# A FiLM transformer block and an expert-choice block: the stretch ahead of the attention loop rebuilt

## The chip, the core and the metric

The kernel runs on one core of a Trainium2 chip. The metric is the device time of one launch in microseconds (us), the median of the runs shown. Smaller is better. The engines are called PE (TensorE), ACT (ScalarE), DVE (VectorE), POOL (GpSimd) and SP (SyncE, which only issues transfers here). Each runs its own instructions in order and waits on semaphores.

## The reference, cut to what matters

```python
# x: (2, 512, 128) float32; cond: (2, 128). Block 0, 128 wide, one head:
h = film(rmsnorm(x, norm1_w), cond, film1_w, film1_b)        # x * (1 + scale) + shift
attn = softmax((h @ q_w + q_b) @ (h @ k_w + k_b).T * D ** -0.5)
x = x + attn @ (h @ v_w + v_b) @ proj_w + proj_b
h = film(rmsnorm(x, norm2_w), cond, film2_w, film2_b)
x = x + gelu(h @ mlp_w1 + mlp_b1) @ mlp_w2 + mlp_b2
# Block 1, 16 heads of 64:
h = ln(x, ln1_g, ln1_b) + silu(cond) @ W_ada.T + b_ada
q, k, v = split(h @ Wqkv.T)                                   # Wqkv: (3 * 16 * 64, 128)
q, k = ln(q, qn_g, qn_b), ln(k, kn_g, kn_b)                   # over the 64 of a head
x = x + attention(q, k, v) @ Wout.T
# then: gate, each of 8 experts takes its 128 best tokens, ln, two layers, scatter-add
```

Since a query or key is layer-normed over its 64 entries, the kernel takes the mean out of the weights: each 64 rows of `Wqkv` of a head are centred once, and only the squares are left to do for each token.

## The kernel before, in words

Everything stays on chip. The 1024 tokens are 8 chunks of 128 (4 for each batch). The program has four parts.

1. Block 0. `x_in` arrives on ACT's queue and right behind it, on the same queue, `wqkv_raw` (1.5 MB); SP issues the rest, the small rows of vectors first, then `film1`, `wq0`, `wk0`, `wv0` and so on. The norm goes: square on ACT (`square`), sum on DVE (`sum_squares`), power -0.5 on POOL (`norm_scale`), product on DVE (`scaled`), transpose on PE (`turn_norm`), FiLM on ACT for batch 0 and on DVE for batch 1 (`into_h`). The same path serves norm 0, 1 and 2. Then q, k and v of both batches, and a loop over the 8 chunks g: `scores0` on PE, maximum on DVE, exponential on ACT, division on DVE, `turn0` on PE, copy on ACT, `mix0` on PE. Then `proj0` of each batch.
2. The weights of block 1 and the MLP of block 0. `make_weights` transposes `Wqkv` and `Wout` in halves of 64 rows (16 transposes for each of four parts m); ACT copies each bank to `w_all` or `wout_T`; DVE sums for the means (`wmean`), POOL subtracts them, DVE casts the whole to `w_hi` (fp32r) and takes the rest `w_lo` for the first half of the heads (POOL does the other half in the loop). Between, PE does the MLP: four `up0` for each batch, each with a gelu on ACT, then `down0`. `block_out` on DVE adds the result to `x_mid` and centres it.
3. The loop of block 1. A piece p is 256 tokens of 2 heads: `project` (three fp32r products in two halves), squares, sums, power -0.5 on POOL, norm, `turn_piece`; a step is 128 query rows of 2 heads: `scores`, maximum, exponential, `turn_probs`, `mix`. Pieces run ahead of the steps; the first five stand ahead of the loop in an order written by hand.
4. Gate, choice by digits, experts, scatter.

PE's order is written out by hand everywhere, and PSUM's eight banks are handed on by semaphores. Sum of squares for norm 1 of batch 1 waits for the projection of batch 1, which waits for `attended0(1)`.

## Time and profile before

| | |
|---|---|
| median of 3 runs | 410.34 us (408.14 to 410.5) |
| the profiled execution | 409.49 us, of which its span (first to last instruction) is 407.8 us |
| PE busy | 365.3 us, 90% of the span |
| ACT, DVE, POOL busy | 268.2, 258.9, 154.9 us |
| mean granted clock of PE | 0.939 of full speed |
| DMA | 9.74 MB |

All times below are from the start of the span. A matmul's row starts when PE begins to read; with a dependent wait the next engine starts some 0.2 us after the end of PE's work, other engines some 0.04 us after each other. Two rows of PE one after the other overlap: the distance of their starts is what the first costs.

### The profile page before, as it was taken

The numbers are of one execution on the slowest core, as the hardware profiler recorded it, in microseconds if no ns is written. First come the engines' busy times: TensorE is split into PE (matmuls) and PEld (weight loads), VectorE is DVE, ScalarE is ACT, GpSimd is POOL, SyncE is SP. The second block draws the span as 40 slices with busy tenths as digits, with TensorE's granted clock in tenths as the row PEclk, the third lists the DMA queues.
The fourth block names the chain that finished last, engine by engine and source line by source line (L and its number), as shares of the span: only waits on it lengthen the run. The fifth ranks groups of instructions, "written<-read, shape, count | busy, mean of one in ns | idle before, by whom it ended". The sixth has DMA issues, their size and how long they took to land.

```text
span 407.8 us, 8743 instructions
## 1 busy us (share of the span) xinstructions
PE 365.3 (90%) x3118; PEld 256.1 (63%) x3118; DVE 258.9 (63%) x596; ACT 268.2 (66%) x655; POOL 154.9 (38%) x159
## 2 busy tenths in 40 slices
PE   0999796676999999999999999999999876799995
PEld 0658555634666676666666766666655555588894
DVE  2466646436876867767768677677686548890333
ACT  2245544349787887887878899978896527256431
POOL 4200431416757546456465464565642011000000
PEclk9999899569999999999999999999999985579999
DMA  8500000000005800000000000000000000000001
GB/s 229 160 2 0 3 0 0 2 0 0 2 3 159 308 0 2 2 2 2 1 2 2 2 3 2 0 2 2 2 2 2 0 2 0 2 2 0 2 0 51
DMA packets 7518, 9.74 MB, mean 24 GB/s; under 512 B 379, under 2 KB 4278, under 8 KB 7478
## 3 DMA queue, kind: packets, MB, share of 16 engines
q1 hardware_dynamic: 5654, 7.11, 5.7%
q10 hardware_dynamic: 1824, 2.10, 1.8%
q8 instruction: 25, 0.41, 0.4%
q14 instruction: 15, 0.12, 0.1%
HBM read 8.68 MB, written 0.52 MB: 23 GB/s over the span
## 4 chain that ended last, share of the span: by engine, by line
PE 81%; DVE 7%; ACT 5%; DMA 2%; issue 2%; POOL 2%; SPq 0%; DVEq 0%; ACTq 0%
PE bank L1318 15%; PE pair L1269 8%; PE pair L1247 8%; PE bank L1070 8%; PE bank L1269 7%; PE bank L1285 6%; PE pair L1285 4%; PE bank L1296 4%; DMA film<-in_L_cond_film_w_dram 2%; PE bank L1210 2%; PE pair L1219 2%; PE bank L1465 2%; PE pair L1305 2%; PE pair L1070 1%; PE pair L1387 1%
## 5 line engine op out<-in xcount | busy, mean ns | idle before, releaser
L424 POOL TENSOR_TENSOR qk_rstd<-qk_ms,minus_half 128x8 f32<-128x8 f32 x32 | 52.5, 1640 | 103.2 <-DVE qk_ms L860 103.2
L1285 PEld LDWEIGHTS bank<-ident,probs 64*128 64x128 f32 x512 | 36.8, 138 | 46.6 <-issue 46.4
L1318 PE MATMUL bank<-probs_T,v_s 128*64 128x256 f32 x512 | 62.3, 385 | 0.6 <-DVE x_att L903 0.6
L872 DVE TENSOR_REDUCE negmax<-pair 128x1 f32<-128x512 f32 x64 | 43.8, 686 | 25.5 <-PE pair L1269 25.5
L598 ACT ACTIVATE probs_T<-bank 128x512 f32<-128x512 f32 x64 | 38.0, 594 | 24.3 <-PE pair L1285 24.1
L589 ACT ACTIVATE probs<-pair,negmax 128x512 f32<-128x512 f32 x64 | 44.0, 687 | 9.6 <-DVE negmax L872 9.4
L1285 PE MATMUL bank<-ident,probs 64*128 64x64 f32 x512 | 43.4, 225 | 2.2 <-DVE probs_T L880 1.3
L1285 PE MATMUL pair<-ident,probs 64*128 64x64 f32 x512 | 45.1, 228 | 0.0
L1318 PEld LDWEIGHTS bank<-probs_T,v_s 128*64 128x64 f32 x512 | 34.1, 136 | 16.5 <-issue 0.8
L880 DVE COPY probs_T<-pair 128x512 f32<-128x512 f32 x64 | 43.7, 682 | 1.2 <-PE pair L1285 1.2
L872 DVE TENSOR_REDUCE negmax<-bank 128x1 f32<-128x512 f32 x64 | 43.6, 683 | 0.0
L589 ACT ACTIVATE probs<-bank,negmax 128x512 f32<-128x512 f32 x64 | 43.6, 694 | 0.0
L1269 PE MATMUL pair<-keys_T,queries_T 64*128 64x512 f32 x128 | 37.1, 656 | 2.0 <-ACT queries_T L581 2.0
L1285 PEld LDWEIGHTS pair<-ident,probs 64*128 64x128 f32 x512 | 36.9, 139 | 0.0
L1269 PE MATMUL bank<-keys_T,queries_T 64*128 64x512 f32 x128 | 36.2, 632 | 0.6 <-ACT probs L589 0.6
L903 DVE TENSOR_TENSOR x_att<-x_att,bank 128x256 f32<-128x256 f32 x32 | 13.5, 422 | 27.9 <-PE bank L1296 27.9
L431 POOL TENSOR_TENSOR qk_n<-qk_raw,qk_rstd 128x512 f32<-128x512 f32 x29 | 30.3, 1043 | 0.0
L1247 PE MATMUL pair<-w_hi,h_hi 128*128 128x384 f32 x64 | 25.3, 396 | 5.0 <-DVE h_lo L841 3.1
L418 POOL TENSOR_TENSOR qk_sq<-qk_raw 128x512 f32<-128x512 f32 x28 | 29.1, 1041 | 0.0
L562 ACT ACTIVATE qk_raw<-pair 128x512 f32<-128x512 f32 x32 | 19.1, 598 | 11.3 <-PE pair L1247 11.3
L437 POOL TENSOR_TENSOR rec_wide<-o_rec,ones 128x256 f32<-128x256 f32 x32 | 19.6, 613 | 14.2 <-DVE o_rec L887 11.4
L894 DVE TENSOR_TENSOR o_T<-bank,rec_T 128x256 f32<-128x256 f32 x32 | 13.6, 425 | 15.2 <-PE bank L1318 15.2
(271 smaller groups left out, 771.6 us busy)
## 6 DMA issues: line engine op xcount, KB each, us to landing
fc_raw<-in_L_cond_fc2s_dram SPq DMA_DIRECT2D x1, 2048.0 KB, 14.9
x_in<-in_x_dram ACTq DMA_DIRECT2D x1, 512.0 KB, 4.1
w<-in_L_cond_mlp_w_dram SPq DMA_DIRECT2D x2, 256.0 KB, 3.6
wout<-in_L_cond_Wout_dram SPq DMA_DIRECT2D x1, 512.0 KB
b_all<-in_L_cond_b2s_dram SPq DMA_DIRECT2D x1, 512.0 KB, 11.1
out_dram<-final SPq DMA_DIRECT2D x2, 256.0 KB, 2.4
film<-in_L_cond_film_w_dram SPq DMA_DIRECT2D x2, 128.0 KB, 5.9
wq<-in_L_cond_q_w_dram SPq DMA_DIRECT2D x1, 64.0 KB, 8.0
```

The lines of the kernel that those rows point to most:

```text
L418: pool.tensor_tensor(qk_sq[:, :, :, :], qk_raw[:, p % 2, :, :, :], qk_raw[:, p % 2, :, :, :], ALU.mult).then_inc(sq_done, 1)
L424: pool.tensor_tensor(qk_rstd[:, :, :].rearrange("p c t -> p (c t)"), qk_ms[:, :, :].rearrange("p c t -> p (c t)"), minus_half[:, 0:8], ALU ...
L431: pool.tensor_tensor(qk_n[:, p % 2, :, :, :], qk_raw[:, p % 2, :, :, :], spread(qk_rstd[:, :, :], [P, 2, 4, HD]), ALU.mult).then_inc(norme ...
L589: act.activation(probs[:, t % 2, h, :], bank[2 * (t % 2) + h][:, :], ACT.Exp, bias=negmax[:, t % 2, h:h + 1], accum_out=row_sum[:, t // 2 ...
L598: act.activation(probs_T[:, r % 2, :, :, at:at + HD], bank[4][:, :].rearrange("p (h k n) -> p h k n", h=2, k=NC), ACT.Copy).then_inc(copie ...
L872: dve.tensor_reduce(negmax[:, t % 2, h:h + 1], bank[2 * (t % 2) + h][:, :], AX, ALU.max, negate=True)\
L880: dve.tensor_copy(probs_T[:, r % 2, :, :, at:at + HD], bank[6][:, :].rearrange("p (h k n) -> p h k n", h=2, k=NC)).then_inc(copied_dve, 1)
L1070: last = pe.transpose(dst[:, n * P:n * P + P], s, ident[:, :])
L1247: last = pe.matmul(in_banks(p)[:, c, 0:W2], h_part[:, at:at + P], w_part[:, g, :], start=(n == 0), stop=(n == 2))
L1269: pe.matmul(bank[2 * (t % 2) + h][:, :], queries_T[rows, i % 2, c * P:c * P + P], keys_T[rows, i % 2, :], start=True, stop=True).then_inc( ...
L1285: last = pe.transpose(bank[(4, 6)[q]][:, n * HD:n * HD + HD], probs[rows, t % 2, n // NC, n % NC * P:n % NC * P + P], ident[rows, rows])
L1318: last = pe.matmul(bank[5][h * HD:h * HD + HD, 0:2 * P], v_s[:, m % 4, k, h * HD:h * HD + HD], probs_T[:, r % 2, h, k, :], start=(k == 0), ...
```

## The change: what it does, and the diff

- The start: `wqkv_raw` is issued after the two squares instead of before them. PE runs 24, 6 and 8 transposes of the identity into a bank that nothing reads (`keep_awake`), around the transpose of the early rows and the FiLM products. DVE does FiLM ahead of the silu.
- PE's order of q, k and v: batch 0 first, then `scores0(0)`, then batch 1's products with `scores0(1)` between.
- The weights: two 64x64 blocks `centring` (identity less 1/64) are made on POOL, and q's and k's parts of `Wqkv` are multiplied by them, so that the weights leave PE turned and centred. Each of three parts (`make_weights(k, m)`, at g = 2, 4 and 5 of block 0's attention loop) fills banks 6 and 7; ACT writes `w_hi` straight from PSUM, DVE writes `w_lo` from PSUM less `w_hi`. `w_all`, `wmean`, POOL's subtraction and the parts of `w_lo` in the loop are gone. `Wout` and `Wgate` are turned after the MLP.
- The MLP: `u0` has its own memory, norm 1 of batch 0 and its MLP start while batch 1's attention ends; `proj0(1)` stands behind `up0(0)`; `down0` goes by k outermost, the last k apart, with `turn_norm(1, 1)` and `turn_norm(2, 0)` ahead of it. The bias `mb0` is added for each batch by itself. A load of ACT's gelu table is called ahead of the last `turned0`.
- Ahead of the loop: `turn_piece(0)` before `project(3)`, `turn_norm(2, 1)` behind `turn_piece(1)`; `qk_ms` and `qk_rstd` have two slots, and `piece_ss(1)` and POOL's second power come before batch 1's norm.
- SP's loads of the experts' weights wait for `Wgate`'s copy and no longer for POOL's last needed `w_lo`.

```diff
+        centring = keep("centring", [P, HD])
...
-        mlp_start = early.at
...
-            sp.wait_ge(w_split, 1 + HP // 2)
+            sp.wait_ge(wout_copied, 3)
...
-            pool.wait_ge(consts, 4)
+            for h in range(2):
+                rows = slice(h * HD, h * HD + HD)
+                pool.wait_ge(consts, 4 + h)
+                pool.tensor_scalar(centring[rows, :], ident[rows, rows], 1.0 / HD, None, ALU.subtract)\
+                    .then_inc(consts, 1)
+            pool.wait_ge(consts, 6)
...
+            def mid_bias(b):
+                at = slice(b * NC, b * NC + NC)
+                pool.wait_ge(norm_done, 3 + b)
+                pool.tensor_tensor(x_mid[:, at, :], x_mid[:, at, :], bias(mb0, NC), ALU.add).then_inc(xmb_ready, 1)
+            for b in range(B):
+                norm_scale(1, b, EPS0)
+                mid_bias(b)
...
-                wait(pool, normed, p)
-                pool.tensor_tensor(qk_rstd[:, :, :].rearrange("p c t -> p (c t)"),
-                                   qk_ms[:, :, :].rearrange("p c t -> p (c t)"),
+                wait(pool, normed, p - 1)
...
-            act.dma_start(wqkv_raw[:, :, :], Wqkv.rearrange("(c p) d -> p c d", p=P)).then_inc(wqkv_in, 16)
...
+            act.dma_start(wqkv_raw[:, :, :], Wqkv.rearrange("(c p) d -> p c d", p=P)).then_inc(wqkv_in, 16)
...
+                act.activation(weight_part(w_hi, n), bank[6 + n % 2][:, :].rearrange("p (g d) -> p g d", d=HD),
+                               ACT.Copy).then_inc(w_high, 1)
...
+            into_h(0)
+            key0(0)
+            exp0(0)
+            key0(1)
+            exp0(1)
+            for g in range(2, TC):
+                exp0(g)
+                turned0(g - 2)
+                if g in (2, 4, 5):
+                    first = {2: 0, 4: 2, 5: 4}[g]
+                    weight_high(first)
+                    weight_high(first + 1)
+            act.wait_ge(mid_ready, 1)
+            square(x_mid, 0)
+            turned0(TC - 2)
+            act.activation(table_call[:, 1:2], minus_half[:, 0:1], ACT.Gelu)
+            turned0(TC - 1)
+            into_h(1)
+            gelu0(0)
+            gelu0(1)
+            act.wait_ge(mid_ready, 2)
+            square(x_mid, 1)
+            for n in range(2, 6):
+                gelu0(n)
             act.wait_ge(norm_in, 1)
             square(xn, 0)
-            act.wait_ge(consts, 2)
+            gelu0(6)
+            gelu0(7)
             act.activation(table_call[:, 0:1], minus_half[:, 0:1], ACT.Exp)
             into_h(2)
-            act.wait_ge(norm_in, 2)
-            square(xn, 1)
+            copy_wout(0)
+            copy_wout(1)
+            act.wait_ge(wT_done, SPLIT_BANKS + 3)
+            act.activation(wgate_T[:, :], bank[5][:, 0:E], ACT.Copy).then_inc(wout_copied, 1)
...
+            def weight_low(n):
+                dve.wait_ge(w_high, n + 1)
+                dve.tensor_tensor(weight_part(w_lo, n), bank[6 + n % 2][:, :].rearrange("p (g d) -> p g d", d=HD),
+                                  weight_part(w_hi, n).bitcast(F32), ALU.subtract).then_inc(w_low, 1)
...
+            query0(0)
+            into_h(0)
+            value0(0)
+            maximum0(0)
+            query0(1)
+            normal0(0)
+            maximum0(1)
+            value0(1)
+            for g in range(2, TC):
+                maximum0(g)
+                normal0(g - 1)
                 if g == 2:
                     late_cols()
                 if g == 4:
                     late_affine()
+                if g in (3, 5, 6):
+                    first = {3: 0, 5: 2, 6: 4}[g]
+                    weight_low(first)
+                    weight_low(first + 1)
                 if g == NC + 2:
                     attended0(0)
-                if g == NC + 4:
-                    batch_out0(0)
+            batch_out0(0)
+            normal0(TC - 1)
+            sum_squares(1, 0)
+            scaled(1, 0, x_mid)
             attended0(1)
-            sum_squares(1, 0)
             batch_out0(1)
-            scaled(1, 0, x_mid)
             sum_squares(1, 1)
             scaled(1, 1, x_mid)
             into_h(1)
-            dve.wait_ge(wT_copied, QK_BANKS)
-            link(dve.tensor_reduce(wmean[:, :, :],
...
+            def keep_awake(n):
+                for _ in range(n):
+                    pe.transpose(bank[7][:, 0:P], ident[:, :], ident[:, :])
+            keep_awake(24)
             pe.wait_ge(early_in, 16 * len(early_loads))
             pe.transpose(bank[0][:, 0:EARLY], early_rows[:, :], ident[0:EARLY, 0:EARLY]).then_inc(cols_T, 1)
+            keep_awake(6)
...
+            keep_awake(8)
...
+                    pe.wait_ge(w_low, SPLIT_BANKS)
...
+            def make_weights(k, m):
+                if m == 2:
+                    pe.wait_ge(wout_in, 32)
+                    pe.wait_ge(gelu0_done, B * HC)
+                else:
+                    pe.wait_ge(wqkv_in, 16)
+                    pe.wait_ge(consts, 6)
+                    pe.wait_ge(k0_ready, 2)
+                    pe.wait_ge(v0_ready, 1)
+                    wait(pe, w_low, 2 * k)
+                for c in range(KC):
+                    for h in range(2):
+                        rows = slice(h * HD, h * HD + HD)
+                        dst = bank[(3 if m == 2 else 6) + h][:, c * HD:c * HD + HD]
+                        if m < 2:
+                            last = pe.matmul(dst, wqkv_raw[rows, KC * m + c, :], centring[rows, :],
+                                             start=True, stop=True)
...
+            def down0(b, ks):
+                pe.wait_ge(mid_ready, b + 1)
+                for k in ks:
+                    pe.wait_ge(gelu0_done, HC * b + k + 1)
+                    for c in range(NC):
+                        last = pe.matmul(bank[(7, 0)[b]][:, c * D:c * D + D],
+                                         u0[:, k, (b * NC + c) * P:(b * NC + c + 1) * P], w20[:, k, :],
+                                         start=(k == 0 and c == 0), stop=(k == HC - 1), skip_group_check=True)
+                if k == HC - 1:
+                    last.then_inc(y0_done, 1)
+            turn_norm(0, 0)
+            pe.wait_ge(qkv_in, 48)
+            pe.wait_ge(affine_ready, 1)
+            pe.wait_ge(h_act, 1)
+            query_key0(0, wq0, bank[3])
+            query_key0(0, wk0, bank[5])
+            turn_norm(0, 1)
+            value0(0)
+            scores0(0)
+            pe.wait_ge(h_dve, 1)
+            query_key0(1, wq0, bank[4])
+            scores0(1)
+            query_key0(1, wk0, bank[6])
+            value0(1)
+            for g in range(2, TC + 2):
                 if g < TC:
                     scores0(g)
-                if 2 <= g < TC + 2:
+                if g == 2:
+                    late_turns()
+                if g == NC + 3:
+                    turn0(g - 2)
+                    proj0(0)
+                else:
                     turn0(g - 2)
                 if g >= 3:
                     mix0(g - 3)
-                if g == 1:
-                    late_turns()
                 if g == 3:
                     late_products()
-                if g == NC + 3:
-                    proj0(0)
+                if g in (2, 4, 5):
+                    make_weights(*{2: (0, 0), 4: (1, 1), 5: (2, 3)}[g])
+            turn_norm(1, 0)
+            mix0(TC - 1)
+            up0(0)
             proj0(1)
-
-
...
+            for n in range(1, HC):
+                up0(n)
+            down0(0, range(HC - 1))
             turn_norm(1, 1)
-            pe.wait_ge(mlp_in, 32)
-            pe.wait_ge(h_act, 2)
...
+            down0(0, (HC - 1,))
+            for n in range(HC, 2 * HC):
                 up0(n)
-                if n == 1:
-                    make_weights(3)
...
+            down0(1, range(HC - 1))
             turn_norm(2, 0)
+            down0(1, (HC - 1,))
+            make_weights(3, 2)
+            pe.transpose(bank[5][:, 0:E], wgate[:, :], ident[0:E, 0:E]).then_inc(wT_done, 1)
             pe.wait_ge(h_split, 1)
-            pe.wait_ge(wT_copied, W_BANKS + 1)
...
             project(0)
             project(1)
-            turn_norm(2, 1)
             project(2)
+            turn_piece(0)
             project(3)
-            turn_piece(0)
             project(4)
             turn_piece(1)
+            turn_norm(2, 1)
             scores(0)
             pe.wait_ge(h_dve, 3)
```

## Rows read from the trace of the kernel before

**Rows 1.** Windows: length, busy of PE, PEld, DVE, ACT, POOL, clock, DMA, GB/s.
```profile
...
70.51:88.05 17.54, 11.16 (x43) 9.89 (x43) 6.33 (x12) 7.39 (x16) 6.09 (x5) 0.62 0.00 1
88.05:101.10 13.05, 9.93 (x64) 5.08 (x65) 7.93 (x16) 9.41 (x25) 5.34 (x5) 0.85 0.00 0
101.10:200.00 98.90, 98.80 (x960) 65.75 (x960) 72.23 (x148) 80.41 (x200) 61.02 (x60) 1.00 0.15 49
...
```

**Rows 2.** Chain that ended last, up to 110: start us, length, what.
```profile
...
2.36 7.73 DMA film<-in_L_cond_film_w_dram
...
23.13 1.11 PE pair L1130 x2
...
73.65 1.64 POOL qk_rstd L424
...
88.05 2.13 PE pair L1269 x4
...
107.12 1.04 PE pair L1247 x6
...
```

**Rows 3.** Timeline of PE: start us, length us, line, operands, count, idle before.
```profile
...
13.62 1.92 PE L1117 MATMUL bank<-h_T,wq 128*128 128x512 f32 x2
...
16.92 1.05 PE L1120 MATMUL pair<-wv,h_T 128*128 128x128 f32 x8
...
31.03 0.60 PE L1070 MATMUL bank<-ident,p 128*128 128x128 f32 x4
31.47 1.06 PE L1145 MATMUL bank<-pT,v 128*128 128x128 f32 x8
32.36 1.02 PE L1130 MATMUL pair<-kT,qT 128*128 128x512 f32 x2
33.22 0.60 PE L1070 MATMUL bank<-ident,p 128*128 128x128 f32 x4
...
43.83 0.66 PE L1192 MATMUL bank<-ident,wqkv_raw 64*128 64x64 f32 x16
...
48.53 3.12 PE L1210 MATMUL bank<-h_T,w 128*128 128x512 f32 x4
...
56.75 3.84 PE L1219 MATMUL pair<-w,u 128*128 128x128 f32 x32
...
70.51 0.41 PE L1247 MATMUL pair<-w_hi,h_hi 128*128 128x384 f32 x1 [3.15 <-DVE h_lo L841]
...
77.33 1.12 PE L1070 MATMUL bank<-ident,xn 128*128 128x128 f32 x4 [3.40 <-DVE xn L723]
...
92.39 1.13 PE L1269 MATMUL pair<-keys_T,queries_T 64*128 64x512 f32 x4
...
```

**Rows 4.** Timelines of ACT, then of DVE, same columns.
```profile
...
4.93 1.15 ACT L481 ACTIVATE sq<-x_in 128x512 f32<-128x512 f32 x2 [1.33 <-DMA x_in<-in_x_dram]
...
36.34 0.69 ACT L512 ACTIVATE p<-bank,soft 128x512 f32<-128x512 f32 x1 [0.92 <-DVE soft L793]
...
7.81 0.69 DVE L723 TENSOR_TENSOR xn<-x_in,rstd 128x512 f32<-128x512 f32 x1
...
35.61 0.69 DVE L793 TENSOR_REDUCE soft<-bank 128x1 f32<-128x512 f32 x1 [0.17 <-PE bank L1130]
...
```

**Rows 5.** Groups by line up to 88: count, busy us, mean ns, idle before.
```profile
...
L404 POOL TENSOR_TENSOR w_all<-w_all,wmean 128x2048 f32<-128x2048 f32 x1 | 3.6, 3619 | 2.1 <-DVE wmean L820 2.1
...
L845 DVE TENSOR_TENSOR w_lo<-w_all,w_hi 128x1536 fp32r<-128x1536 f32 x1 | 1.8, 1759 | 0.0
...
```

**Rows 6.** Timeline of PE after the loop: three banks of transposes.
```profile
...
358.04 2.80 PE L1070 MATMUL bank<-ident,fc_raw 128*128 128x128 f32 x12
...
```

**Rows 7.** Windows of PE after the loop, before and after those transposes.
```profile
...
335.00:358.00 23.00, 17.33 (x145) 12.51 (x144) 19.68 (x96) 10.71 (x20) 2.77 (x4) 0.50 0.00 1
358.00:361.50 3.50, 3.50 (x22) 3.31 (x20) 3.15 (x5) 2.08 (x4) 0.00 (x0) 0.50 0.01 2
361.50:380.00 18.50, 18.50 (x127) 15.80 (x125) 7.13 (x7) 11.79 (x25) 0.00 (x0) 1.00 0.00 1
...
```

More of the change, by code:

```diff
@@ L167, in film_attention_then_expert_choice @@
         w_lo = loop("w_lo", [P, HP, W2], F32R)
+        wqkv_raw = Area(loop.at)("wqkv_raw", [P, WC, D])
         qk_raw = loop("qk_raw", [P, 2, 2, 4, HD])
@@ L906, in _ @@
             piece_ss(0)
-            scaled(2, 1, xn)
+            piece_ss(1)
             piece_norm(0)
-            piece_ss(1)
-            into_h(2)
+            sum_squares(2, 1)
             piece_norm(1)
             piece_ss(2)
+            scaled(2, 1, xn)
+            into_h(2)
             piece_norm(2)
@@ L1197, in _ @@
-            for m in range(3):
-                make_weights(m)
-            turn_norm(1, 0)
-            turn_norm(1, 1)
-            pe.wait_ge(mlp_in, 32)
-            pe.wait_ge(h_act, 2)
-            def up0(n):
-                b, c = n // HC, n % HC
-                if n == HC:
-                    pe.wait_ge(h_dve, 2)
-                wait(pe, gelu0_done, n - 1)
-                pe.matmul(bank[3 + n % 2][:, :], w10[:, c * P:c * P + P], h_T[:, b * N:b * N + N],
-                          start=True, stop=True).then_inc(u0_done, 1)
```

261 lines of the change are left out of this document (96 added, 165 removed).

## The prediction

> **What bounds the kernel now.** I read the windows first. In the loop PE is busy 98.80 of 98.90 us at clock 1.00 [rows 1]: PE bounds it, and nothing here touches PE's work in it. Ahead of it the reader is to see the opposite. From 70.51 to 88.05 PE is busy 11.16 of 17.54 us at a mean clock of 0.62, from 88.05 to 101.10 at 0.85 [rows 1]. So this stretch is bound by chains from engine to engine, and PE's gaps are paid a second time, since the clock falls to its lower level (1.2 GHz) behind them and the products that follow take twice as long. Second the chain of waits: its first long piece is one transfer, `film1`, 7.73 us up to 10.09 [rows 2], with `wqkv_raw` in flight beside it. Third PE's own timeline, for checkpoints that exist in both kernels: first q product 13.62 [rows 3], `scores0(2)` 23.13 [rows 2], first `up0` 48.53, `project(0)` 70.51 [rows 3], `scores(0)` 88.05 [rows 2], `scores(2)` 92.39 [rows 3]. What the change is worth is the shift of the last. Behind it the loop is the same work in the same order; POOL loses one operation in each of four iterations, beside a full PE, which is worth nothing.
>
> **Prices.** On PE at the upper clock, from distances of starts [rows 3]: four transposes 0.44 (31.03 to 31.47), four 128x128 products 0.89 (31.47 to 32.36), a 128x512 product 0.86 (32.36 to 33.22), `down0` 3.7, 16 half transposes 0.55. A `project` is 1.04 [rows 2]. A 512-wide operation is 0.69 on DVE (0.60 if the next is ready) and 0.69 on ACT with its accumulator some 0.2 behind [rows 4]; an ACT copy out of PSUM I take at 0.6. POOL's small power is 1.64 [rows 2].
>
> **Part 1, the start: 13.62 becomes 10.5, -3.1.** With `wqkv_raw` issued behind the squares, `film1` no longer shares the engines with it, and the next limits are `x_in` (4.93 now [rows 4]) and DVE: two sums up to 6.8, the copy of the columns, then `scaled(0, 0)` at 7.81 [rows 4], which waits for POOL. FiLM's three small operations 0.6, `into_h` 0.8 with its wait, and q could start at 10.0 if `x_in` lands at 4.6 or so. Against it stands PE's new work: 24 transposes from 1.6 on. They are 0.21 each at the lower clock (358.04, 12 in 2.6 us [rows 6]), so up to 5.1 us, ending at 6.7, when the copy of the columns wants them; then 6 more, the FiLM products and 8 more. At the upper clock the last 14 take 1.5 and lie half beside DVE; at the lower they take 3.0 and lie on the path, q then at 12.7 or later. ACT issues `wqkv_raw` between its squares and the silu's exponential; nobody on the path waits for that one now that DVE does FiLM first, and the first use of `wqkv_raw` is near 19, so its later landing is covered by 5 us or more (7.7 us for the transfers that now share with it [rows 2]). So -3.1, between -3.6 and 0.
>
> **Part 2, q, k, v: -2.1.** Before, from 13.62 to 23.13, 9.5 us, with two 512 products at twice their price (v starts at 16.92, 3.3 behind 13.62 [rows 3], for what takes 1.7 at the upper clock), the late turns 0.6 and a wait of 0.4. After: q, k, transposes, v, `scores0(0)`, q, `scores0(1)`, k, v, which is six times 0.86, 0.44 and two times 0.89, 7.4 us, no wait in it. If the clock is still low, 1.7 comes back.
>
> The question for both parts is whether transposes lift the clock. In the only long run of bare transposes here, 12 from 358.04 on, the clock was 0.50 before and up to 361.50, and 1.00 behind [rows 6, 7]: only 1.0 us of products stood between, while products ran for 3.3 us from 13.62 before they quickened [rows 3]. I read this as: they count. The Trainium skill, "TensorE: Matmul & The Clock Gate", Part 4 (PE-mode transpose), says the full rate does not engage for transposes, which do not count as PE-busy in the same way; by that rule `keep_awake` is only work in the way, and the rival below is its result. Here row and rule differ, and 7 of 10 go to the row.
>
> **Part 3, the attention of block 0 with the weights inside: -0.5.** Removed ahead of the MLP are three parts of `make_weights` (the row at 43.83 is one [rows 3]) and PE's wait for ACT's copies between them. Added are two parts of 16 centring products and one of 16 transposes (0.55). The trace has no 64-column fp32 product. Lower bound the half transposes, 0.55 for 16; upper bound a 128x128 product each, 0.22, so 3.6. A full product takes two instructions for a transpose's one (x8 against x4 in [rows 3]), and the nearest row is the half transposes, so twice these, 1.1. Walking PE's list from `scores0(2)` to `up0(0)`: six scores 5.2, eight `turn0` 3.5, eight `mix0` less one behind the norm's transpose 7.1, late turns and products 1.3, weights 2.75, `proj0(0)` 0.9, `turn_norm(1, 0)` 0.4: 21.2. The waits: the third part needs `w_low(3)`, which DVE reaches after `maximum0(5)` and the division, 1.5 beyond PE's other work; `proj0(0)` needs `w_low(5)` and `attended0(0)` behind it, 0.8; batch 0's norm (sum 0.7, POOL 1.3, product 0.7) shows 1.0; small ones 0.4. Queued behind them on PE are the scores of the next chunk, and ACT's `w_high` keeps `exp0` of the next chunk waiting. Sum 24.9 against 25.4. Per step DVE now has 1.4 and ACT 1.35 of PE's 2.19, and six `w_low` of 0.6 (1.76 for three in [rows 5]) and six `w_high` of 0.5 are spread over three of the steps: cover enough, if the order holds. Bounds -1.6 and +5.
>
> **Part 4, the MLP: 22.0 becomes 18.0, -4.0.** Work of PE: eight `up0` 6.9, `down0` twice 7.4, `proj0(1)` 0.9, two norms' transposes 0.9, `Wout` and gate 0.7: 16.8, and waits 1.2. What goes: 0.6 of v's weights, 1.3 because the first two `up0` came at the lower clock (3.1 for four instructions [rows 3] against 1.7), and of the wait of 3.15 for `h_lo` [rows 3] all but 0.7, since norm 2 of batch 0 now runs beside batch 1's `down0` and `split_h(0)` stands ahead of `block_out(1)` on DVE. POOL's 3.62 over the weights and DVE's work around it [rows 5] go too; they were beside PE and are worth nothing themselves. ACT's two table loads move into the path's neighbourhood: the gelu load stands ahead of `turned0(7)`, covered by PE's `turn0(7)`, `mix0(6)` and the norm's wait; uncovered it costs 1.3.
>
> **Part 5, five pieces ahead of the loop: 17.5 becomes 11.4, -6.1.** PE's work is five `project` 5.2, three times 0.44: 6.5. The waits are 4.9: `turn_piece(0)` is behind square, sum, POOL's 1.64 and the norm, 1.7; then 1.6, 0.9 and 0.7. Before, the transposes for norm 2 of batch 1 stood second in PE's list and cost 3.40 [rows 3], as POOL did 1.64 [rows 2] of the first piece ahead of them; `project(2)` to `project(4)` and both first `scores` then ran at the lower clock. New on DVE is `piece_ss(1)` ahead of the first norm; POOL's second power follows its first without a gap. The added waits, `project(1)` for `att_added` and the first two `turn_piece` for the copies of `Wout` and `Wgate`, have long been met when PE comes there in the walk; late by x they would cost x, with `project(2)` and all of the list behind them.
>
> **Part 6, the first scores: 4.34 becomes 3.0, -1.3**, the clock alone.
>
> **Sum.** -3.1 - 2.1 - 0.5 - 4.0 - 6.1 - 1.3 = -17.1. A walk with every wait at its least is too good; and in part 5 PE idles 4.9 of 11.4 us, so the clock may fall once. I allow 2.0: a fall doubles two to three pieces, 2 to 3 us, in some half of the cases, and 0.1 here and there is lost. So -15.1: 409.5 for the profiled execution (407.8 of it span) becomes 394.4. The median of the runs stands 0.85 above that execution, so the forecast is 395.
>
> **Rivals.**
> - Transposes don't lift the clock. For it the rule above, and that FiLM's products and eight transposes between 10.09 [rows 2] and 13.62 did not speed the first q. Against it rows 6 and 7. Price: q at 13.0 to 13.6 instead of 10.5, 1.7 and more in part 2, and one more fall ahead of the loop: +6, 401. Chance 0.25.
> - The weights bind the attention loop. Each part goes PE 1.1, two `w_high` 1.0, two `w_low` 1.3, and the next use of banks 6 and 7 waits for it. If centring products cost 0.22 each (+5), or each of three rounds is waited for in full (3.4 each against 2.3 counted for all): +5 to +8, 402. For it: the two waits that the walk already finds; against it: 0.8 us of slack for ACT and DVE in each step. Chance 0.15.
> - Slower: the clock stays low through the whole of block 0. PE's work there is 21.2 and 16.8 us, each microsecond at the lower level costs one more, so it decides once more than 19 us of it run low; all of it gives 395 + 38 = 433. It would need a rule by which small and half-height work keeps the level down, as in the digits' part, where PE is busy 17.33 of 23.00 at 0.50 [rows 7]. Against it: products as wide as here lifted the clock each time. Chance 0.02.
> - The shift is given back in the loop or the tail. The experts' loads come earlier, PE is full there anyway. Chance 0.03, 405 to 410.
>
> **Chances and range.** The forecast has 0.55 (389 to 399). For 8 in 10 the range takes in the first two rivals: 389 to 403. A median of this kernel can tell 1%, 4 us, from no change. Faster by over 1%: 0.94, within 1%: 0.04, slower: 0.02.
>
> **What the profile after would show.** First q product near 10.5 and `film1` gone from the chain of waits; the 512 products 0.86 apart from the first on; 25 us from `scores0(2)` to `up0(0)` with one wait of PE for DVE's `w_lo` of 1.5; clock 1.00 from 40 to 60; `project(0)` near 61, `scores(0)` near 73, and from there the same distance to the end as before. Wrong would be: first 512 products 1.7 apart (rival one), centring products over 0.1 each or PE waiting over 3 us for `w_lo` (rival two), or a clock of 0.5 in the windows before `scores(0)`.

## The result, and the profile after

The changed kernel takes 395.75 us (median of 4 runs, 395.59 to 397.12) where the kernel before took 410.29 beside it: a ratio of 0.967, with a 95% interval of 0.963 to 0.971. Its profiled execution took 395.64, 393.9 of it span, against 407.8 of span before. The sum in the prediction was 394.4 for that execution, the forecast 395.

Windows of the changed kernel, from the first `up0` to `project(0)`, from there to the first `scores`, and of the loop (columns as in [rows 1]):

```profile
...
44.71:62.63 17.92, 17.45 (x113) 12.55 (x114) 8.41 (x14) 9.16 (x15) 3.68 (x5) 1.00 0.00 1
62.63:74.02 11.39, 7.54 (x42) 6.31 (x43) 7.74 (x15) 8.35 (x20) 6.38 (x5) 1.00 0.00 0
...
77.41:200.00 122.59, 119.26 (x1156) 79.17 (x1157) 88.87 (x182) 100.17 (x250) 70.93 (x68) 1.00 0.12 40
...
```

PE is busy 7.54 of 11.39 us in the five pieces ahead of the loop, at clock 1.00, where [rows 1] has 11.16 of 17.54 at 0.62. The work is the same five pieces, so the 3.6 us that PE's busy time fell by is the clock, and PE idles 3.85 instead of 6.4. The loop itself is the same: from the first mix to the last it takes 221.60 before and 221.73 after (325.97 less 104.37, 311.10 less 89.37).

PE's timeline of the changed kernel, whose rows answer to [rows 3]:

```profile
...
1.57 5.20 PE L1089 MATMUL pair<-ident 128*128 128x128 f32 x24 [1.57 <-POOL minus_half L366]
...
7.94 1.07 PE L1089 MATMUL pair<-ident 128*128 128x128 f32 x8
8.85 0.60 PE L1081 MATMUL pair<-ident,xn 128*128 128x128 f32 x4
10.41 1.10 PE L1131 MATMUL bank<-h_T,wq 128*128 128x512 f32 x2 [0.96 <-ACT h_T L484]
11.34 1.02 PE L1131 MATMUL bank<-h_T,wk 128*128 128x512 f32 x2
...
17.86 1.02 PE L1145 MATMUL pair<-kT,qT 128*128 128x512 f32 x2
...
26.93 2.00 PE L1191 MATMUL pair<-centring,wqkv_raw 64*128 64x64 f32 x32
28.86 1.12 PE L1145 MATMUL bank<-kT,qT 128*128 128x512 f32 x2
...
32.72 0.71 PE L1196 MATMUL pair<-ident,wqkv_raw 64*128 64x64 f32 x16 [1.40 <-DVE w_lo L791]
...
37.66 1.16 PE L1170 MATMUL pair<-wp,oT 128*128 128x128 f32 x8 [0.54 <-DVE oT L796]
...
43.09 0.66 PE L1081 MATMUL pair<-ident,xn 128*128 128x128 f32 x4 [0.72 <-DVE xn L721]
...
44.71 1.10 PE L1207 MATMUL bank<-h_T,w 128*128 128x512 f32 x2
...
62.63 0.41 PE L1279 MATMUL pair<-w_hi,h_hi 128*128 128x384 f32 x1 [0.46 <-DVE h_lo L854]
...
65.36 0.44 PE L1279 MATMUL pair<-w_hi,h_hi 128*128 128x384 f32 x1 [0.41 <-ACT v_s L562]
...
68.03 0.66 PE L1081 MATMUL bank<-ident,qk_n 128*128 128x128 f32 x4 [1.35 <-DVE qk_n L877]
...
71.16 0.45 PE L1279 MATMUL pair<-w_hi,h_hi 128*128 128x384 f32 x1 [1.42 <-ACT v_s L562]
...
74.02 1.13 PE L1303 MATMUL pair<-keys_T,queries_T 64*128 64x512 f32 x4 [0.68 <-ACT queries_T L577]
...
77.41 1.13 PE L1303 MATMUL pair<-keys_T,queries_T 64*128 64x512 f32 x4 [0.81 <-ACT probs L585]
...
```

The reader is to see three things. The first two 512 products start 0.93 apart (10.41, 11.34), and the eight idle transposes ahead of them take 0.91 to the next start (7.94, 8.85), 0.11 each: both at the upper clock, where [rows 3] has 3.3 us for two products. The centring products cost 1.93 for 16 (two instructions each, 26.93 to 28.86). And PE still waits ahead of the loop, but never for more than 1.42, where it waited 3.15 and 3.40 before [rows 3].

The steps of the prediction against this trace (us):

| from, to | before | predicted | after |
|---|---|---|---|
| start to first q | 13.62 | 10.5 | 10.41 |
| to `scores0(2)` | 9.51 | 7.4 | 7.45 |
| to `up0(0)` | 25.40 | 24.9 | 26.85 |
| to `project(0)` | 21.98 | 18.0 | 17.92 |
| to `scores(0)` | 17.54 | 11.4 | 11.39 |
| to `scores(2)` | 4.34 | 3.0 | 3.39 |
| to the end of the span | 315.41 | 315.4, and 2.0 allowed | 316.49 |

### The profile page after: what moved, and what is told of

Its sections match the earlier page's. It is cut to its first block, busy times and chain, and to the rows that moved or that the text cites. A ratio compares the mean times of both kernels' runs of the same rounds, so it can differ in the third digit from the quotient of the medians.

```text
span 393.9 us, 8921 instructions
## 1 busy us (share of the span) xinstructions
PE 365.6 (93%) x3188; PEld 260.2 (66%) x3188; DVE 256.0 (65%) x596; ACT 267.2 (68%) x656; POOL 148.6 (38%) x157
## 4 chain that ended last, share of the span: by engine, by line
PE 83%; DVE 7%; ACT 5%; issue 2%; POOL 1%; DVEq 0%; POOLq 0%; ACTq 0%
PE bank L1352 15%; PE pair L1303 8%; PE pair L1279 7%; PE bank L1303 7%; PE bank L1081 7%; PE bank L1319 6%; PE pair L1319 4%; PE bank L1330 4%; PE bank L1207 2%; PE bank L1499 2%; PE pair L1089 2%; PE pair L1081 2%; PE pair L1339 2%; PE pair L1215 2%; PE pair L1421 1%
## 5 line engine op out<-in xcount | busy, mean ns | idle before, releaser
L1303 PE MATMUL pair<-keys_T,queries_T 64*128 64x512 f32 x128 | 36.1, 641 | 2.4 <-ACT queries_T L577 1.6
L1303 PE MATMUL bank<-keys_T,queries_T 64*128 64x512 f32 x128 | 35.2, 617 | 0.6 <-ACT probs L585 0.6
L1279 PE MATMUL pair<-w_hi,h_hi 128*128 128x384 f32 x64 | 24.3, 379 | 2.3 <-ACT v_s L562 1.8
L428 POOL TENSOR_TENSOR rec_wide<-o_rec,ones 128x256 f32<-128x256 f32 x32 | 19.6, 612 | 14.2 <-DVE o_rec L897 11.4
```

What stands on the lines that cost most here:

```text
L1279: last = pe.matmul(in_banks(p)[:, c, 0:W2], h_part[:, at:at + P], w_part[:, g, :], start=(n == 0), stop=(n == 2))
L1303: pe.matmul(bank[2 * (t % 2) + h][:, :], queries_T[rows, i % 2, c * P:c * P + P], keys_T[rows, i % 2, :], start=True, stop=True).then_inc( ...
```

## The experiments

All changes are to the changed kernel unless the text says that they are to the kernel before. Intervals are those of the ratio to the kernel before, whose median beside these runs was 408.9 to 410.2; so the ratios are what to compare (the change alone: 0.967). The checkpoints of each profiled execution, from PE's timeline (first mix is the first product of probabilities with values in the loop):

| run | first q | `scores0(2)` | `up0(0)` | `project(0)` | `scores(0)` | first mix | span | ratio |
|---|---|---|---|---|---|---|---|---|
| before | 13.62 | 23.13 | 48.53 | 70.51 | 88.05 | 104.37 | 407.8 | 1 |
| after | 10.41 | 17.86 | 44.71 | 62.63 | 74.02 | 89.37 | 393.9 | 0.967 |
| no_awake | 10.56 | 19.67 | 46.52 | 64.44 | 75.82 | 91.18 | 395.4 | 0.974 |
| awake_24 | 10.25 | 19.38 | 46.23 | 64.15 | 75.54 | 90.89 | 395.4 | 0.974 |
| wqkv_first | 15.10 | 24.21 | 51.06 | 68.98 | 80.36 | 95.71 | 399.5 | 0.979 |
| before_wqkv | 11.12 | 21.16 | 46.49 | 68.80 | 86.11 | 102.40 | 406.5 | 0.996 |
| before_both | 10.88 | 18.81 | 44.15 | 64.96 | 82.00 | 98.28 | 402.3 | 0.990 |
| plain_weights | 9.98 | 17.43 | 41.70 | 59.63 | 71.02 | 86.37 | 389.7 | 0.957 |
| late_third | 10.86 | 18.31 | 43.52 | 61.44 | 72.83 | 88.19 | 392.1 | 0.960 |
| reordered | 10.06 | 17.51 | 44.37 | 62.29 | 72.67 | 88.03 | 392.5 | 0.963 |
| old_order | 10.44 | 17.89 | 44.74 | 62.67 | 81.42 | 97.73 | 401.3 | 0.983 |
| mlp_behind | 10.13 | 17.58 | 51.49 | 70.11 | 81.52 | 96.88 | 400.5 | 0.985 |
| both_orders | 10.62 | 18.07 | 43.27 | 61.20 | 71.58 | 86.93 | 391.6 | 0.960 |
| awake_moved | 10.12 | 17.57 | 42.77 | 60.69 | 72.05 | 87.40 | 390.6 | 0.960 |

Two things must be known to read it. Among the seven profiled executions with the same start (after, plain_weights, late_third, reordered, old_order, mlp_behind, both_orders) the first q wanders from 9.98 to 10.86, so distances between checkpoints say more than positions. It goes with how soon the clock rises inside the 24 idle transposes: they take 4.39, 4.55 and 4.70 us where the first q comes at 9.98, 10.06 and 10.13, and 5.20 to 5.38 where it comes at 10.41 to 10.86. The earliest of them, plain_weights:

```profile
...
1.57 4.39 PE L1089 MATMUL pair<-ident 128*128 128x128 f32 x24 [1.57 <-POOL minus_half L366]
...
8.37 0.66 PE L1081 MATMUL pair<-ident,xn 128*128 128x128 f32 x4
...
```

Here the norm's transposes start at 8.37, where the changed kernel's start at 8.85 behind the eight idle ones. The distances repeat to 0.02 where nothing was touched: `up0(0)` to `project(0)` is 17.92 or 17.93 in ten of the runs. And behind the first mix the time to the end is between 303.2 and 304.7, by where the clock falls after the loop (end of the section on the prediction).

### Do idle transposes lift the clock?

**no_awake.**

```diff
-            keep_awake(24)
...
-            keep_awake(6)
...
-            keep_awake(8)
```

> The changed kernel without its 38 idle transposes at the start (24, 6 and 8). Theory, transposes lift the clock: the norm's transposes no longer stand behind the eight (they started at 8.85 though xn was ready at 8.25), so the first q product comes 0.4 to 0.6 earlier, near 9.9; but the first two to three 512 products are 1.7 apart instead of 0.86 and v's eight small ones slower as well: +2 to +2.6 by the second chunk's scores. Net +1.5 to +2: 397.3 to 397.8 us. Rival, the transposes do nothing for the clock and the products quicken by themselves: 512 products 0.86 apart from the first on, and the kernel is 0.5 faster than with them, 395.3.

Measured 398.05 us, ratio 0.974 (0.970 to 0.977). PE's timeline of it:

```profile
...
8.48 1.12 PE L1081 MATMUL pair<-ident,xn 128*128 128x128 f32 x4 [0.52 <-DVE xn L721]
10.56 2.05 PE L1128 MATMUL bank<-h_T,wq 128*128 128x512 f32 x2 [0.96 <-ACT h_T L484]
12.39 1.78 PE L1128 MATMUL bank<-h_T,wk 128*128 128x512 f32 x2
14.01 0.60 PE L1081 MATMUL bank<-ident,xn 128*128 128x128 f32 x4
...
```

The two products start 1.83 apart and the next comes 1.62 behind, against 0.93 and 0.86. From first q to `scores0(2)` it is 9.11 against 7.45: 1.66 for the clock, the 1.7 of the prediction's part 2. The first q itself isn't earlier, as was expected (9.9), for the norm's four transposes now take 1.12 instead of 0.60 and end as late. So the first rival falls, and the transposes are worth 1.8 us at the first mix and 2.3 to 2.6 in the medians and ratios.

The prediction weighed a rule of the Trainium skill, "TensorE: Matmul & The Clock Gate", Part 4 (PE-mode transpose), by which the full rate does not engage for transposes. This pair of runs speaks against it: the same products run at about twice the pace behind the 38 transposes. So do the transposes themselves, 0.21 each at first and 0.11 each in the burst of eight.

**awake_24.** Only the first 24.

```diff
-            keep_awake(6)
...
-            keep_awake(8)
```

> The changed kernel with the first 24 idle transposes only, without the 6 and the 8 behind. Theory, the 24 do the lifting and the other 14 are work in the way: the norm's transposes start at 8.3 instead of 8.85, q 0.5 earlier, products 0.86 apart from the first on: 395.2 us. Rival, the clock needs the others too: between 6.8 and 10 PE has only 1 us of work, the clock is down again at the first q product, and 1.7 comes back: 397.

397.79 us, ratio 0.974 (0.969 to 0.978): the rival. Its timeline:

```profile
...
8.63 0.66 PE L1081 MATMUL pair<-ident,xn 128*128 128x128 f32 x4 [0.56 <-DVE xn L721]
10.25 1.33 PE L1129 MATMUL bank<-h_T,wq 128*128 128x512 f32 x2 [0.96 <-ACT h_T L484]
11.38 1.91 PE L1129 MATMUL bank<-h_T,wk 128*128 128x512 f32 x2
13.08 1.06 PE L1081 MATMUL bank<-ident,xn 128*128 128x128 f32 x4
...
```

At 8.63 the clock is up (0.66 for four transposes), in the middle of q it falls, and the k product takes 1.70 to the next start. All that the 24 had bought is lost: it is 9.13 to `scores0(2)`, as with none. The 14 behind them are needed.

### What is the place of the Wqkv load worth?

**wqkv_first**, the load issued ahead of the squares, all else as changed:

```diff
             act.dma_start(x_in[:, :, :], x.rearrange("b (c p) d -> p (b c) d", p=P)).then_inc(x_loaded, 16)
+            act.dma_start(wqkv_raw[:, :, :], Wqkv.rearrange("(c p) d -> p c d", p=P)).then_inc(wqkv_in, 16)
             act.wait_ge(x_loaded, 16)
...
-            act.dma_start(wqkv_raw[:, :, :], Wqkv.rearrange("(c p) d -> p c d", p=P)).then_inc(wqkv_in, 16)
```

> The changed kernel with the Wqkv load issued ahead of the squares again, as before the change. Theory, the two loads shared the DMA engines and film1 was the path: film1 lands near 10 again, the first q product is at 13.3 instead of 10.4, and PE has nothing between 7.7 and 10, so the clock is down for the first two 512 products: +2.9 and +1.7, 400.3 us. Rival A, the transposes before and behind FiLM keep the clock up over that gap: +2.9 alone, 398.6. Rival B, the order of issue is worth nothing, the transposes took the gain: 395.7, q at 10.4.

400.9 us, ratio 0.979 (0.975 to 0.983), near the 400.3 of the theory. But the first q comes at 15.10, 1.8 later than the 13.3 expected, and `film1` is not what was late. Timeline and windows:

```profile
...
8.69 0.27 PE L1093 MATMUL pair<-ident,early_rows 7*128 7x7 f32 x1 [2.73 <-DMA early_rows<-in_L_cond_k_b_dram]
...
11.34 1.95 PE L1089 MATMUL pair<-ident 128*128 128x128 f32 x8
...
15.10 2.05 PE L1131 MATMUL bank<-h_T,wq 128*128 128x512 f32 x2 [0.96 <-ACT h_T L484]
...
```

```profile
...
6.00:8.70 2.70, 0.01 (x1) 0.01 (x1) 0.92 (x2) 0.13 (x1) 1.96 (x4) 0.91 1.05 298
8.70:15.00 6.30, 5.38 (x23) 4.59 (x23) 2.34 (x9) 0.98 (x2) 1.30 (x2) 0.50 0.73 173
...
```

In this execution PE waited for the small rows (`early_rows`, 8.69; 5.24 to 5.36 is when PE could read them in before_wqkv and no_awake, and 6.03 in the kernel before, which issues the `Wqkv` load as early), and not for `film1` behind them. Why they came so much later than at 6.03 is not shown. PE had nothing for 2.7 us, the granted clock went to 0.50, and the other 14 transposes ran at half pace. So the transposes alone buy nothing: first q to `scores0(2)` is 9.11, as without them.

**before_wqkv**, the opposite edit to the kernel before (the load moved behind the squares), and **before_both**, that and the three calls of `keep_awake`.

> The kernel before, with only the Wqkv load issued behind the two squares. Theory: film1 lands near 7.5, the first q product comes 2.9 to 3.2 earlier (10.6), still at the lower clock, and all that follows shifts by the same: 410.3 - 3.1 = 407.2 us. Rival: the weights' later landing or the order on DVE (silu ahead of the first norm) eats part of it: 408 to 409.

> The kernel before with the Wqkv load issued behind the squares and with the 24, 6 and 8 transposes at the start, nothing else. Theory, the transposes lift the clock: beside the 3.1 of the load, the first two 512 products are 0.86 apart instead of 1.7, -1.7, less 0.4 because the eight stand in the norm's way: 410.3 - 4.4 = 405.9 us. Rival: transposes do nothing for the clock: 407.2 to 407.7, first products 1.7 apart.

408.17 us, ratio 0.996 (0.994 to 0.999), where 407.2 was expected: the rival's range. And 404.56, ratio 0.990 (0.986 to 0.993). Their first q products:

```profile
...
11.12 1.91 PE L1117 MATMUL bank<-h_T,wq 128*128 128x512 f32 x2
...
```

```profile
...
10.88 1.02 PE L1126 MATMUL bank<-h_T,wq 128*128 128x512 f32 x2
...
```

The load alone brings the first q 2.50 forward, but from there to `scores0(2)` it takes 10.04 instead of 9.51, the clock being down for longer, and 1.97 is left at the first mix, 1.3 of span. So the load alone is worth 0.7 us by the medians and 1.5 by the ratio, not 3.1. With the transposes it is 4.32 at `scores0(2)` and 6.09 at the first mix; nearly all of the growth is the clock in two stretches (`up0(0)` to `project(0)` 20.81 instead of 21.98, `project(0)` to `scores(0)` 17.04 instead of 17.54). The 4.3 of the medians lies near the 4.4 expected.

### What did the centring products cost?

**plain_weights**, queries and keys not centred:

```diff
-                            last = pe.matmul(dst, wqkv_raw[rows, KC * m + c, :], centring[rows, :],
-                                             start=True, stop=True)
+                            last = pe.transpose(dst, wqkv_raw[rows, KC * m + c, :], ident[rows, rows])
```

> The changed kernel with plain transposes in place of the 64 centring products (so queries and keys are not centred: that part of the computation is left out). Theory, the products are on PE's path and were mis-sized: two times 1.93 becomes two times 0.55, and the stretch from the second chunk's scores to the first up0 falls from 26.85 to 24.1 or so; 2.5 us less for the kernel, 393.2. Rival, DVE and ACT (six w_hi, six w_lo) are what binds and PE would only wait longer for them: under 1 us less, with larger waits of PE for w_lo and for the quotient.

391.82 us, ratio 0.957 (0.953 to 0.961), and 24.27 from `scores0(2)` to `up0(0)` instead of 26.85.

```profile
...
19.33 0.71 PE L1191 MATMUL pair<-ident,wqkv_raw 64*128 64x64 f32 x16
19.97 1.12 PE L1145 MATMUL bank<-kT,qT 128*128 128x512 f32 x2
...
29.71 0.71 PE L1195 MATMUL pair<-ident,wqkv_raw 64*128 64x64 f32 x16 [1.40 <-DVE w_lo L791]
...
```

16 transposes are 0.64 and 16 products 1.93; twice 1.29 is 2.58, the whole difference in this stretch. The median fell by 3.9, more than the 2.5 expected: at the first mix it is 3.00, of which 0.43 is this run's start, and the rest lies behind the loop. PE's wait for `w_lo` stays at 1.40: the products are on the path with their full length, and ACT and DVE follow them.

### Where does PE wait, and does an order help?

**late_third.**

```diff
                     turn0(g - 2)
+                if g == NC + 2:
+                    make_weights(2, 3)
                 if g >= 3:
                     mix0(g - 3)
...
-                if g in (2, 4, 5):
-                    make_weights(*{2: (0, 0), 4: (1, 1), 5: (2, 3)}[g])
+                if g in (2, 4):
+                    make_weights(*{2: (0, 0), 4: (1, 1)}[g])
```

> The changed kernel with the third part of the weights moved in PE's list behind scores0(6) and turn0(4), where it stood ahead of them and waited 1.40 us for DVE's w_lo. Theory, that wait is filled by 1.3 us of work: up0(0) 1.0 to 1.4 earlier, 394.6 us. Rival, ACT's w_hi and DVE's w_lo of that part come later by as much and the wait moves to the batch's projection and the mix behind it: no change, 395.7.

393.66 us, ratio 0.960 (0.957 to 0.964). From `scores0(2)` to `up0(0)` 25.21, 1.64 less, more than the 1.0 to 1.4 expected: the 1.40, and 0.35 of the wait for the projection of batch 0 (0.54 in the changed kernel), less 0.11 elsewhere:

```profile
...
33.17 0.71 PE L1196 MATMUL pair<-ident,wqkv_raw 64*128 64x64 f32 x16
...
36.46 1.16 PE L1170 MATMUL pair<-wp,oT 128*128 128x128 f32 x8 [0.19 <-DVE oT L796]
...
```

**reordered.** PE turns piece 1 ahead of `project(4)`; ACT copies piece 3 ahead of piece 0's affine step.

```diff
-            for p in range(2, 4):
-                piece_raw(p)
-                piece_square(p)
-                piece_affine(p - 2)
+            piece_raw(2)
+            piece_square(2)
+            piece_raw(3)
+            piece_affine(0)
+            piece_square(3)
+            piece_affine(1)
...
-            project(4)
             turn_piece(1)
+            project(4)
```

> The changed kernel with three steps exchanged ahead of the loop: PE turns piece 1 ahead of project(4), and ACT copies piece 3 out of PSUM ahead of both affine steps of piece 0. By the trace PE waited 1.42 for that copy and 0.68 for the queries. Theory, the path from there into the loop is this chain: scores(0) at 72.7 instead of 74.0 and all behind it 1.3 us earlier, 394.4. Rival, the loop's first products wait for something else (POOL's small powers, the exponentials): scores(0) comes earlier and the loop's first mix stays where it was, 395.7.

394.31 us, ratio 0.963 (0.959 to 0.967). `project(0)` to `scores(0)` 10.38 instead of 11.39, and the first mix 1.34 earlier, of which 0.35 is this run's start:

```profile
...
70.35 0.44 PE L1281 MATMUL pair<-w_hi,h_hi 128*128 128x384 f32 x1 [0.41 <-ACT v_s L562]
...
72.67 1.13 PE L1305 MATMUL pair<-keys_T,queries_T 64*128 64x512 f32 x4 [0.55 <-ACT queries_T L577]
...
```

The wait for `v_s` fell from 1.42 to 0.41. 1.0 of the expected 1.3 came.

**old_order.** The order of before in the five pieces:

```diff
-            project(2)
-            turn_piece(0)
-            project(3)
-            project(4)
-            turn_piece(1)
-            turn_norm(2, 1)
+            turn_norm(2, 1)
+            project(2)
+            project(3)
+            turn_piece(0)
+            project(4)
+            turn_piece(1)
```

and on POOL `norm_scale(2, 1)` ahead of `piece_scale(1)`, on ACT `square(xn, 1)` ahead of the pieces, on DVE the sums and norms as before.

> The changed kernel with the order of before in the five pieces ahead of the loop, on PE, POOL, DVE and ACT (batch 1's norm first, its transposes second in PE's list). Theory, the order carries most of part 5: PE waits some 5 us for the norm with nothing behind it, the clock falls, and the projects and the first scores run at half rate: scores(0) 5 to 6 later, its distance to scores(2) back to over 4; 402 us. Rival, part 5 came from the clock that was up already when PE got there and not from the order: 396 to 397.5.

403.23 us, ratio 0.983 (0.978 to 0.988):

```profile
...
70.71 1.12 PE L1081 MATMUL bank<-ident,xn 128*128 128x128 f32 x4 [5.71 <-DVE xn L721]
71.47 0.67 PE L1279 MATMUL pair<-w_hi,h_hi 128*128 128x384 f32 x1
...
81.42 2.08 PE L1303 MATMUL pair<-keys_T,queries_T 64*128 64x512 f32 x4 [1.11 <-ACT queries_T L577]
...
```

PE waits 5.71 for the norm, the clock falls, and `scores(0)` is 18.75 behind `project(0)`, where it was 17.54 before the change. In this stretch PE idles 8.69 instead of 3.85 and is busy 10.06 instead of 7.54, at a mean clock of 0.73. The first mix comes 8.36 later. So the order on the four engines, which was undone only as a whole, carries all of part 5; the rival, a clock that is up already when PE gets there, would have left it near 11.4. It is worth more here than the difference of the two kernels, since the norm of batch 1 starts later against `project(0)` than it did: DVE writes its centred input (`xn`) 1.41 behind `project(0)` (64.08), before the change 1.90 ahead of it (68.61).

**mlp_behind.** Batch 0's MLP behind batch 1's norm:

```diff
             mix0(TC - 1)
-            up0(0)
             proj0(1)
-            for n in range(1, HC):
+            turn_norm(1, 1)
+            for n in range(0, HC):
                 up0(n)
-            down0(0, range(HC - 1))
-            turn_norm(1, 1)
-            down0(0, (HC - 1,))
+            down0(0, range(HC))
...
             into_h(1)
-            gelu0(0)
-            gelu0(1)
             act.wait_ge(mid_ready, 2)
             square(x_mid, 1)
+            gelu0(0)
+            gelu0(1)
```

> The changed kernel with batch 0's MLP behind batch 1's projection and norm, as before the change: on PE mix0(7), proj0(1), turn_norm(1, 1) and only then up0(0) to up0(3) and down0(0), on ACT the square of batch 1 ahead of the first gelu. Theory, that overlap is worth what PE then waits for with nothing behind it, output, square, sum, POOL and norm of batch 1, some 4.2 us: project(0) 4 to 4.5 later, and 1 more where the clock falls over that wait: 400 to 401 us. Rival, part 4 came from the weights' parts and the second norm's place, and the work behind fills the wait: under 1.5 us later, 397.

402.57 us, ratio 0.985 (0.980 to 0.990), about two more than expected:

```profile
...
50.58 1.12 PE L1081 MATMUL bank<-ident,xn 128*128 128x128 f32 x4 [4.28 <-DVE xn L721]
51.49 6.16 PE L1207 MATMUL bank<-h_T,w 128*128 128x512 f32 x8
...
```

The wait is 4.28 for 4.2 expected. The clock falls over it: the four `up0` behind it take 5.99 (51.49 to 57.48), where batch 1's four in the changed kernel take 3.72. From `scores0(2)` to `project(0)` it is 52.53 instead of 44.77; PE idles 8.20 instead of 3.22 of this, and its work takes 2.8 longer. Before the change the same two stretches took 47.38.

### The version that beats both

**both_orders**, late_third and reordered together.

> The changed kernel with both new orders, that of late_third and that of reordered. Theory: they lie in different stretches of one chain and add up, up0(0) 25.2 behind the second chunk's scores and scores(0) 10.4 behind project(0): 2.6 us less than the changed kernel, 393.1 us. Rival: the loop's first products then wait for something else and half of it is lost: 394.4.

392.54 us (6 runs, 391.64 to 393.84), ratio 0.960 (0.956 to 0.963), 0.6 under the 393.1 expected: 25.20 and 10.38 in their two stretches, so they add up there. All six runs are faster than the four of the changed kernel (395.59 to 397.12). By the ratio it is not told apart from late_third, also 0.960; that `reordered` adds its 1.0 rests on the profiled stretches.

**awake_moved**, that and the third burst split:

```diff
-            keep_awake(8)
+            keep_awake(3)
...
             turn_norm(0, 0)
+            keep_awake(7)
```

> The kernel of both_orders with the third burst of eight idle transposes split: three where it stood and seven behind the norm's transposes, in the 0.96 us in which PE waits for h_T. Theory, the burst stood in the norm's way by 0.5 and the clock wants the work, not its place: the norm's transposes start 0.5 earlier, the products stay 0.86 apart from the first, and the kernel is 0.5 faster than both_orders, 392.0 us. Rival A, the clock falls over the start and 1.7 comes back: 393.8. Rival B, the seven end later than h_T is ready and take the gain back: 392.5.

392.75 us, ratio 0.960 (0.957 to 0.964): not told apart from both_orders. In the profiled executions the norm's transposes start at 8.51 instead of 9.06, the first q at 10.12 instead of 10.62, and it is 7.45 to `scores0(2)`. But that does not show the theory: its 24 transposes took 4.52, those of both_orders 5.38, and mlp_behind, with the eight unsplit, has 8.51 and 10.13 as well, behind 24 in 4.70. That the clock rose sooner inside the 24 is enough for the 0.5. In part 5 this execution lost more, 11.36 instead of 10.38. Windows of awake_moved, then of both_orders, over PE's wait for piece 0 and the 4 us behind it:

```profile
...
64.60:66.09 1.49, 0.14 (x1) 0.00 (x0) 1.12 (x4) 0.76 (x2) 1.49 (x2) 1.00 0.00 0
66.09:70.09 4.00, 3.89 (x15) 3.40 (x16) 2.73 (x5) 2.64 (x7) 3.90 (x4) 0.57 0.00 0
...
```

```profile
...
65.10:66.60 1.50, 0.16 (x2) 0.00 (x1) 1.13 (x4) 0.77 (x2) 1.50 (x2) 1.00 0.00 0
66.60:70.60 4.00, 3.59 (x22) 3.11 (x23) 2.73 (x5) 3.62 (x9) 3.90 (x4) 1.00 0.00 0
...
```

The same program there, the same wait of 1.35 and 1.34: in one the clock fell behind it, in the other not. Whether the split gains anything stays open.

## Why the prediction was right, point by point

- **Part 1, the start (-3.1, measured -3.2).** Right, and no_awake, wqkv_first and before_wqkv show its conditions: the moved load brings the first q 2.5 forward by itself, and the rows of the early loads belong to it as much as `film1`. That idle transposes can stand on the path is also so: in the changed kernel the norm's transposes start behind the eight. Where the clock rose sooner inside the 24 they do not wait for them (8.37 in plain_weights). Without the last 14, 1.7 comes back in part 2 (awake_24).
- **Part 2, q, k, v (-2.1, measured -2.06).** Right for the reason given: without the transposes 1.66 comes back. That they lift the clock was given 7 of 10, on one row of twelve transposes. The likeliest rival, with 0.25, is refuted; its price of 6 was also too high, for no_awake costs 2.6 at most. The two other places where it was to cost something (q later, one more fall ahead of the loop) didn't appear.
- **Part 3, the attention of block 0 (-0.5, measured +1.45).** This step failed, and one term of it: "the nearest row is the half transposes, so twice these, 1.1" for 16 centring products. They are 1.93, 1.66 more for the two parts. A row was at hand that would have come nearer: a 128x128 product is 0.22, and half its columns is 0.11, 1.8 for 16; the number of rows that it sums over (64) saves nothing. "Centring products over 0.1 each" was named as a sign of being wrong, and they are 0.12. The stretch missed by 1.95, and the other 0.3 is a difference of two misses: the three named waits are 1.40, 0.54 and 0.72, 0.64 less than listed (1.5, 0.8, 1.0), while distances of starts that are 0.1 to 0.2 over their price (0.96 for a `scores0` at 28.86, priced at 0.86), for which the sum had 0.4, come to some 1.4. By the windows PE idles 2.75 of the stretch in both kernels (before: 22.65 busy of 25.40, in the lines below; after: 24.10 of 26.85), so the stretch grew by work alone.
- **Part 4, the MLP (-4.0, measured -4.06).** Right in sum. Nearly all of it is idle time, as the windows of the kernel before and of the changed one show: PE idled 4.17 of 21.98 (second line below) and idles 0.47 of 17.92, with the wait for `h_lo` down from 3.15 to 0.46. Two misses cancel: PE's work, put at 16.8, is 17.45, and the waits, put at 1.2, are 0.47. mlp_behind does not test these terms: its wait for `h_lo` is 0.47 too, and only 0.7 of what it costs lies in this stretch. The other 7.1 lies ahead of the first `up0`. It shows that with the weights' parts gone from there the overlap is needed; no run takes the terms of part 4 apart.

```profile
...
23.13:48.53 25.40, 22.65 (x187) 18.09 (x187) 15.37 (x40) 14.44 (x32) 3.30 (x5) 0.98 0.01 2
48.53:70.51 21.98, 17.81 (x102) 11.38 (x102) 13.72 (x18) 11.05 (x17) 6.30 (x4) 0.95 0.00 0
...
```

- **Part 5, five pieces (-6.1, measured -6.15).** Right in sum, and old_order shows that it is the order. That the sum fits to 0.05 is luck, for two misses cancel in it: the waits were listed as 1.7, 1.6, 0.9 and 0.7, 4.9 in all, and are 1.35, 1.42, 0.68 and 0.41, 3.86; PE's work, put at 6.5 by distances of starts, is 7.54, since each piece that a wait interrupts also shows its own run-out.
- **Part 6 (-1.3, measured -0.95).** The clock is 1.00 as forecast, and the two `scores` take 1.92 instead of 3.71. That alone is 1.8 and not 1.3; then PE waits 0.81 for the exponential where no wait was counted.
- **The allowance of 2.0** was for a fall of the clock, which didn't come in the profiled execution. The miss of part 3 used it up, so that the total came out as near as it did by luck. The profiled execution (395.64) is 1.2 above its forecast (394.4), about the 1.1 behind the loop for which nothing was counted; the median is only 0.8 above 395, because it stands 0.1 above that execution and not 0.85. That a fall of the clock in part 5 can come and cost about 1 was seen in awake_moved.
- **Rival two, the weights bind the attention loop,** named two prices. Products at 0.22 would have brought 5; they are 0.12. Three rounds waited for in full would have brought the rest; PE waited once for `w_lo`, 1.4, as the forecast had it. The stretch missed by 1.95 and not by 5 to 8, and late_third takes 1.64 back.
- **Rivals three and four.** The clock is 1.00 through block 0 from the first q on, by the spacing of its products. Nothing is given back in the loop: from the first mix to the last the two kernels keep their distance of 15.0 to 0.13 (104.37 and 89.37, 325.97 and 311.10).

The 1.1 between the shift at `scores(2)` (15.0) and that of the span (13.9) arose behind the loop. In the changed kernel the clock fell at the router's second products, a little earlier in PE's list:

```profile
...
316.54 1.42 PE L1363 MATMUL pair<-wgate_T,xa_T 128*128 128x8 f32 x8 [0.79 <-DVE xa_T L959]
317.81 1.09 PE L1081 MATMUL pair<-ident,fc_raw 128*128 128x128 f32 x4
...
```

The four transposes that take 1.09 here took 0.63 before, and the rise behind the digits came later too, which makes up for the rest. Kernels with the same list of PE show from 303.2 to 304.7 here (the kernel before 303.4, with other starts 304.0 and 304.1), so no cost of the change is seen in this.

## What to carry to other kernels

Where PE is fed by chains from engine to engine, look at the granted clock of each stretch first: a wait is paid once as idle time and again in the products behind it. Undoing the order of the pieces cost 7.4 us up to `scores(0)`, 4.8 of it idle time and 2.5 slower work, and 1.0 more behind. Idle transposes kept the clock up over the short start of this kernel, where the waits ahead of the first products came down to one of 0.96; with two more, of 0.26 and 0.56, and fewer transposes between (awake_24), or with one of 2.73 (wqkv_first), it fell. Price a small fp32 product by its columns from the nearest full product, not from a transpose of the same shape. And before a difference of 0.5 us at the start is put down to an edit, see in each execution where the clock rose.

## What the runs showed of the hardware that was not expected

- Transposes alone lift PE to its upper level, and not at a fixed place: the 24 at the start took 5.20 us in the changed kernel and 4.15 in before_both, whose clock rose inside them. Not always so soon: in wqkv_first the granted clock stayed at 0.50 from 8.70 to 15.00, with PE busy 5.38 of 6.30 us, most of it with transposes.
- The clock can fall soon behind a rise. In awake_24 PE ran at the upper level at 8.63 and at the lower at 11.38, with one wait of 0.96 between and one of 0.56 ahead.
- At the same wait in the same list it fell in one execution (awake_moved, 0.57 behind a wait of 1.35) and not in another (both_orders, 1.00 behind 1.34). What decides it was not found.
- Ahead of its first rise the granted clock in the records doesn't show the lower level: no_awake's products at 10.56 and 12.39 run at half pace, and its window gives the clock as 1.00. There the distance of starts tells it, not the clock. Behind a first rise a fall is shown (0.50 in wqkv_first). The window of no_awake:

```profile
...
8.48:14.01 5.53, 4.57 (x8) 2.12 (x9) 2.27 (x8) 0.78 (x1) 3.20 (x2) 1.00 0.98 248
...
```
